# Windowed differential attention in an eight-sublayer kernel: q's spreads in the loop through the small banks and VectorE, and k with swapped k as one projection

## The chip, the cores and the metric

The kernel runs on one core of a Trainium2 chip. The metric is the device time of one launch in microseconds; the lower the better. A core has TensorE (PE: matmuls into PSUM, and PEld, its weight loads), VectorE (DVE), ScalarE (ACT), GpSimd (POOL) and SyncE (SP), which issues the transfers here. Each engine works through its own program in order and waits on semaphores that others raise. PSUM has eight banks of 128 x 512 float32; GpSimd has no work on them in this kernel.

## The reference

Four attention and four feed-forward sublayers follow each other on x of 1024 tokens x 256 features, each with a residual and a layer norm. Only the third one, with grouped keys and a window of 64, is touched by the change:

```python
q = (x @ Wq).reshape(b, s, N_HEADS, HEAD_DIM).transpose(0, 2, 1, 3)   # 16 heads of 16
k = (x @ Wk).reshape(b, s, N_KV, HEAD_DIM).transpose(0, 2, 1, 3)      # 4 heads of 16
v = (x @ Wv).reshape(b, s, N_KV, HEAD_DIM).transpose(0, 2, 1, 3)
q = q * cos + rotate_half(q) * sin
k = k * cos + rotate_half(k) * sin
q1, q2 = (q[..., :SUB], q[..., SUB:])                                  # SUB = 8
k1, k2 = (k[..., :SUB], k[..., SUB:])
a1 = jnp.einsum('bhqd,bhkd->bhqk', q1, k1) * scale                     # + window mask
a2 = jnp.einsum('bhqd,bhkd->bhqk', q2, k2) * scale                     # + window mask
p1, p2 = softmax(a1), softmax(a2)
diff = relu(p1 - lam[None, :, None, None] * p2)
diff = diff / (diff.sum(axis=-1, keepdims=True) + 1e-06)
out = jnp.einsum('bhqk,bhkd->bhqd', diff, v)
return out @ Wo
```

## The kernel before

**PSUM.** Three single banks, bank0 to bank2, form the small ring (`r_slot`): TensorE fills a slot and raises `r_full`, VectorE empties it and raises `r_free`; TensorE may be three slots ahead. Two pairs of banks, pair0 and pair1, form the big ring (`e_slot`): TensorE fills, ScalarE empties (`e_full`, `e_free`), two slots ahead. One bank, `pvb`, takes the products with v. Inside the loop of the windowed sublayer the two pairs are counted by `w_full` and `w_free` instead, over the items of `W_RING`.

**Rotation (items R).** The tokens are split in two halves of 512. `W_HALVES` lists six pieces: k for both halves, then q's two tiles of eight heads for the first half, then for the second. For each piece, `tile_rows(i, 0)` projects it and `tile_rows(i, 1)` projects it once more with swapped halves of each head (the weights lie side by side as wq, swapped wq, wk, swapped wk), each into a bank. VectorE multiplies the one by the cosine and the other by the sine (`rotate`, line 1237) and adds them (line 1241). For q these are 128 rows, for k 64. The sum is then cut into three bf16 parts: ScalarE rounds it (`highest`, line 922), VectorE subtracts and rounds again (`middle`, lines 1257 and 1258), GpSimd takes the rest (`lowest`, line 787). The buffers of the sum alternate between two.

**Spreads (items s).** `spread` (line 1695) multiplies the three parts by 0/1 selectors of 32 rows and so lays two heads (of q, or of k) out over 128 rows, in the pattern of parts that a bf16 product of float32 precision needs: six matmuls of 32 x 128 x 512 for two banks. Ahead of the loop, and in it, they take a slot of the big ring, and ScalarE copies both banks at once to bf16 (lines 937 and 944).

**The loop.** A unit is a block of 128 queries and a group of four heads; there are 8 x 4, in the order of `UNITS`. For unit k: TensorE fills both banks of a pair with the masked scores of a1 and a2 (S, lines 1742 and 1748); VectorE takes the negated maxima (line 1288); ScalarE writes the exponentials and their sums, four heads a bank (line 955); VectorE forms the ratio of the sums (`ratio`, lines 1269 and 1270); GpSimd scales the second half and subtracts (lines 804 and 807); three units later TensorE transposes the result into the small ring (uT, line 1757), from where VectorE takes it with a relu (line 1300). After four units TensorE multiplies with v (line 1774), ScalarE copies the sums (line 961), TensorE transposes them (line 1781) and VectorE divides (lines 1310 to 1312). The output projection, residual and norm of the first half (lines 1498 and 1316, 1493, 1056 to 1090) run in the later units.

**The order** is the list `W_BEFORE` and then `W_PLAN`, both from `windowed_plan`; every engine walks the same lists and takes its items. Before the loop: k's pieces, v of the half that is there first, the transposes of the other half of x (`x1`), the pieces of k and of the first half of q, then the spreads of k and of q's group 0. In the loop, behind the scores of units 0, 1 and 2: the two spreads of q's groups 1, 2 and 3 each; behind unit 3: v of the other half; behind 4 to 7: the pieces of q of the second half; behind 8 to 15: one spread each of the second half of q. On VectorE the ratio of unit k-1 stands behind the maxima of unit k, then the item of the list, then the relu of unit k-3.

## Time and profile before

| | us |
|---|---|
| median of 3 runs | 1169.01 |
| lowest and highest | 1168.03, 1169.27 |
| the profiled execution | 1170.22 |
| its span | 1168.5 |
| busy in the span: TensorE, VectorE, ScalarE, GpSimd | 1006.3, 699.4, 540.4, 331.8 |
| mean granted TensorE clock | 0.896 |

The rows below come from the one profiled execution. Times count from the start of the span. In a row of the timeline the first number is the start, the second the length in time (for a merged row from the first start to the last end), then engine, line, operation, the tile written <- the tiles read, partitions and elements, and how many; the brackets give how long the engine was idle before it and what ended that.
### The profile page before, as it was taken

Reading aid. Unit: us, or ns where it says so; the run is one execution under the profiler, and the core shown is the slowest. Engines: PE = TensorE matmul, PEld = TensorE weight load, DVE = VectorE, ACT = ScalarE, POOL = GpSimd, SP = SyncE. Lnnn points to the kernel's source line nnn. Section 1 sums busy time; section 2 is a strip of 40 time slices with the busy share of each in tenths; the row PEclk is TensorE's granted clock in tenths of the full one; section 3 lists DMA queues with packets and bytes.
Section 4 is the critical chain, followed back from the end, with each engine's and each line's share of the span. In section 5 each row is a group of like instructions: output and inputs, shape, how many; then the busy total and the mean of one; then the engine's idle time right before and its main releaser. Section 6 shows DMA issues by size and latency. Waiting matters only on the chain. (4 is left out here: it accounts for less than half of the span.)

```text
span 1168.5 us, 16473 instructions
## 1 busy us (share of the span) xinstructions
PE 1006.3 (86%) x5922; PEld 570.2 (49%) x5922; DVE 699.4 (60%) x1985; ACT 540.4 (46%) x1145; POOL 331.8 (28%) x464
## 2 busy tenths in 40 slices
PE   6999998788699886899999899997757988888785
PEld 2544454674254454437438444444444544445575
DVE  1667773776166794632432567777291688876665
ACT  3566655331768873210110556664304365555422
POOL 3211112331257773000000321112461154532223
PEclk8989998999576786899999889999877899999888
DMA  6000000103000000200000020000000000000000
GB/s 229 1 1 1 1 1 1 50 1 160 1 18 1 1 2 1 106 0 1 1 0 1 1 87 23 1 1 1 1 1 0 1 1 1 1 1 1 1 19 19
DMA packets 4325, 21.61 MB, mean 18 GB/s; under 512 B 377, under 2 KB 1657, under 8 KB 3220
## 3 DMA queue, kind: packets, MB, share of 16 engines
q1 hardware_dynamic: 4244, 20.55, 4.6%
q8 instruction: 48, 0.79, 0.3%
q14 instruction: 33, 0.27, 0.1%
HBM read 19.01 MB, written 1.05 MB: 17 GB/s over the span
## 5 line engine op out<-in xcount | busy, mean ns | idle before, releaser
L897 ACT ACTIVATE PB<-pair 128x1024 f32<-128x1024 f32 (+3 forms) x288 | 223.3, 812 | 135.3 <-PE pair L1621 133.8
L1139 DVE CUSTOM_DVE_ANT_0 junk<-bank,cst 128x128 bf16<-128x128 f32 (+3 forms) x384 | 171.3, 488 | 114.4 <-PE bank L1605 112.0
L730 POOL TENSOR_SCALAR_AFFINE_SELECT PB<-PB 128x256 f32<-128x256 f32 x192 | 79.0, 414 | 327.5 <-ACT PB L897 325.4
L1142 DVE TENSOR_REDUCE pmx<-bank 128x1 f32<-128x512 f32 x192 | 122.8, 685 | 55.9 <-PE bank L1605 54.9
L1605 PE MATMUL bank<-KO_r,QO_r 64*128 64x512 f32 (+3 forms) x576 | 140.2, 417 | 11.1 <-DVE A L1217 3.9
L1637 PE MATMUL pvb<-PB,V 128*32 128x512 f32 (+3 forms) x1152 | 125.3, 507 | 10.8 <-ACT PB L897 8.0
L1605 PEld LDWEIGHTS bank<-KO_r,QO_r 64*128 64x128 f32 x576 | 71.5, 189 | 113.6 <-DVE pmx L1139 38.9
L1617 PE MATMUL pair<-QO_r,KO_r 64*128 64x512 f32 (+3 forms) x576 | 114.4, 388 | 12.7 <-ACT PB L897 11.5
L736 POOL TENSOR_TENSOR parts_r<-y_f,parts_r 128x512 fp32r<-128x512 f32 x24 | 30.8, 1282 | 313.0 <-ACT parts_r L868 313.0
L955 ACT ACTIVATE KO<-pair,nm 128x128 f32<-128x128 f32 x256 | 90.1, 395 | 32.4 <-DVE nm L1288 32.3
L1621 PE MATMUL pair<-ms,sel_r 64*128 64x512 f32 (+3 forms) x576 | 101.1, 343 | 0.0
L1617 PEld LDWEIGHTS pair<-QO_r,KO_r 64*128 64x128 f32 x576 | 55.3, 186 | 62.9 <-ACT PB L897 50.1
L977 ACT ACTIVATE PB<-pair 128x512 f32<-128x512 f32 (+1 forms) x28 | 16.7, 597 | 125.3 <-PE pair L1493 125.3
L1056 DVE TENSOR_TENSOR X<-bank,X 128x256 f32<-128x256 f32 x56 | 23.7, 424 | 81.8 <-PE bank L1876 43.9
L804 POOL TENSOR_SCALAR KO<-KO,cc,cst 128x128 f32<-128x128 f32 x128 | 55.7, 450 | 50.0 <-DVE cc L1270 49.4
L1493 PE MATMUL pair<-xT,WA 128*128 128x512 f32 x96 | 61.6, 784 | 9.1 <-DMA WA<-in_w_att 7.7
L1288 DVE TENSOR_REDUCE nm<-pair 128x4 f32<-128x512 f32 x64 | 42.4, 686 | 31.4 <-PE pair L1748 31.0
L955 ACT ACTIVATION_READ_ACCUMULATOR KO<-pair,nm 128x1 f32 x256 | 60.3, 236 | 0.0
L1621 PEld LDWEIGHTS pair<-ms,sel_r 64*128 64x128 f32 x576 | 56.8, 187 | 3.8
L1493 PE MATMUL pair<-xT,WF 128*128 128x512 f32 (+1 forms) x112 | 56.8, 631 | 0.0
L1424 DVE TENSOR_TENSOR PB<-bank,PB 128x512 f32<-128x512 f32 (+1 forms) x28 | 19.4, 691 | 60.8 <-PE bank L1493 60.7
L1493 PE MATMUL bank<-xT,WF 128*128 128x512 f32 (+1 forms) x112 | 55.1, 616 | 0.0
(205 smaller groups left out, 1688.7 us busy)
## 6 DMA issues: line engine op xcount, KB each, us to landing
WF<-in_moe_gu SPq DMA_DIRECT2D x1, 3520.0 KB, 10.8
WA<-in_w_att SPq DMA_DIRECT2D x3, 1024.0 KB, 10.7
WF<-in_tern_w SPq DMA_DIRECT2D x1, 3072.0 KB, 9.8
V<-in_moe_d SPq DMA_DIRECT2D x1, 1792.0 KB, 7.5
xT<-in_xT SPq DMA_DIRECT2D x2, 512.0 KB, 5.8
X<-in_x SPq DMA_DIRECT2D x1, 1024.0 KB, 10.6
A<-in_rope SPq DMA_DIRECT2D x1, 1024.0 KB, 4.7
out<-X SPq DMA_DIRECT2D x2, 512.0 KB, 2.9
```

Of the source, the lines that this page charges most:

```text
L730: pool.affine_select(p2, p2, pattern=[[0, 2], [1, P]], compare_op=ALU.is_ge, fill=0.0, base=0, channel_multiplier=-1).then_inc(causal, 1)
L804: last = pool.tensor_scalar(e2[:, hh, :], e2[:, hh, :], cc[:, k % 4, 1, hh:hh + 1], lam, ALU.mult, ALU.mult)
L897: act.activation(pb[:, st % 2, 2 * i:2 * i + 2, 0:n], ps[:, :, 0:n], ACT.Exp, scale=scale)\
L955: last = act.activation(ew[k % EW][:, z, hh, :], slot[:, z, hh * P:(hh + 1) * P], ACT.Exp, bias=nm2[:, (2 * k + z) % 4, hh:hh + 1], accum_ ...
L1139: r_done(dve.tensor_tensor_reduce(junk[:, (r_used - 1) % 3, 0:n], ps[:, 0:n], tri[:, HALF - n:HALF], 1.0, LOWEST, ALU.add, ALU.max, accum_ ...
L1142: r_done(dve.tensor_reduce(to, ps[:, 0:n], AX.X, ALU.max))
L1288: dve.tensor_reduce(nm2[:, (2 * k + z) % 4, :], pair[(n // 2 - 1) % 2][:, z, :].rearrange("p (h n) -> p h n", h=HG), AX.X, ALU.max, negate ...
L1493: last = pe.matmul(ps, w(c), x(c), start=(c == 0), stop=(c == ND - 1))
L1605: pe.matmul(r_slot()[:, 0:n], qd[rows, TWO * g + i, t * P:(t + 1) * P], kd[rows, TWO * g + i, c * HALF:c * HALF + n], start=True, stop=Tru ...
L1617: pe.matmul(ps[:, j, 0:n], kd[rows, TWO * g + i, kb * P:(kb + 1) * P], qd[rows, TWO * g + i, q0:q0 + n], start=True, stop=False)
L1621: last = pe.matmul(ps[:, j, 0:n], sel_r[rows, 2 * TWO + i, :], ms[rows, b, q0 - qh * HALF:q0 - qh * HALF + n], start=False, stop=True)
L1637: last = pe.matmul(pvb[j * STRIP:(j + 1) * STRIP, q0 - qh * HALF:HALF], v_all[:, kb, g * HG + j, :], pb[:, st % 2, j, 0:n], start=(kb == 0 ...
```

## The change

1. In the loop, a spread of q takes two slots of the small ring instead of one of the big ring, and VectorE copies each bank (`q_rows`, two `tensor_copy`) instead of ScalarE the pair. The big ring holds only scores there. Scores that need freshly spread rows wait on `r_free`.
2. q's group 1 of the first half is spread ahead of the loop, also through the small ring. The other items move up by one unit: groups 2 and 3 behind units 0 and 1, v behind 2, the rotations behind 3 to 6, the spreads of the second half behind 7 to 14.
3. k and swapped k are projected by one matmul of 128 columns of weights instead of two of 64, for each half; VectorE multiplies rows 0 to 63 by the cosine and rows 64 to 127 by the sine into rows 0 to 63, with a wait between the two.
4. Ahead of the loop, the spreads of k's first half stand right behind the second projection of k, those of its other half behind q's pieces; `middle` of the last piece stands behind the copies of group 0.

```diff
--- before.py
+++ after.py
@@ -399,13 +399,16 @@
     def rows(side, g, half):
         return [("s", side, g, x, half) for x in range(TWO)]
 
-    before = [("R", 0, 0), ("R", 0, 1), ("v", W_SOON), ("x1",)] + [("R", i, k) for i in (1, 2, 3) for k in range(2)] \
-        + rows("k", 0, W_SOON) + rows("k", 0, W_LATE) + rows("q", 0, W_OUT)
-    late = {0: rows("q", 1, W_OUT), 1: rows("q", 2, W_OUT), 2: rows("q", 3, W_OUT), 3: [("v", W_LATE)],
-            4: [("R", 4, 0)], 5: [("R", 4, 1)], 6: [("R", 5, 0)], 7: [("R", 5, 1)]}
+    def q_rows(g, half):
+        return [("q", g, x, half) for x in range(TWO)]
+
+    before = [("R", 0, 1), ("v", W_SOON), ("x1",), ("R", 1, 1)] + rows("k", 0, W_SOON) \
+        + [("R", i, k) for i in (2, 3) for k in range(2)] + rows("k", 0, W_LATE) + rows("q", 0, W_OUT) + q_rows(1, W_OUT)
+    late = {0: q_rows(2, W_OUT), 1: q_rows(3, W_OUT), 2: [("v", W_LATE)],
+            3: [("R", 4, 0)], 4: [("R", 4, 1)], 5: [("R", 5, 0)], 6: [("R", 5, 1)]}
     for g in range(NG):
         for x in range(TWO):
-            late[8 + TWO * g + x] = [rows("q", g, W_END)[x]]
+            late[7 + TWO * g + x] = [q_rows(g, W_END)[x]]
     plan = []
     for k in range(len(UNITS) + 3):
         if k < len(UNITS):
@@ -432,7 +435,7 @@
 
 PLANS = {s: attention_plan(s) for s, kind in enumerate(SUBLAYERS) if kind == ATT}
 W_BEFORE, W_PLAN = windowed_plan()
-W_RING = [item for item in W_PLAN if item[0] in ("S", "s")]
+W_RING = [item for item in W_PLAN if item[0] == "S"]
 
 
 def w_banks(item):
@@ -469,7 +472,7 @@
 
     n = R_ATT + R_GLU
     for item in W_BEFORE + W_PLAN:
-        n += {"R": 1, "v": 1, "uT": 1, "accT": 1, "outT": ND, "proj": 1}.get(item[0], 0)
+        n += {"R": 1, "v": 1, "q": 2, "uT": 1, "accT": 1, "outT": ND, "proj": 1}.get(item[0], 0)
         if item == ("uT", gi):
             return n
 
@@ -938,10 +941,6 @@
                 for item in W_PLAN:
                     if item[0] == "R" and item[2]:
                         highest(item[1])
-                    if item[0] == "s":
-                        n = w_banks(item)
-                        act.wait_ge(w_full, n)
-                        act.activation(spread_to(item), pair[(n // 2 - 1) % 2][:, :, :], ACT.Copy).then_inc(w_free, 2)
                     if item[0] == "S":
                         k = item[1]
                         t, g = UNITS[k]
@@ -1231,15 +1230,26 @@
                     tile, half = W_HALVES[i]
                     rows, sc = (P, SUB ** -0.5) if tile < 2 else (KV * HD, 1.0)
                     x = w_buf[i % 2]
-                    if i >= 2 and k == 0:
+                    if i >= 2 and k == (tile == 2):
 
                         dve.wait_ge(w_lo, i - 1)
-                    r_done(dve.scalar_tensor_tensor(x[0:rows, k, :], r_slot()[0:rows, :], sc,
-                                                    rope[0:rows, k, half * HALF:(half + 1) * HALF], ALU.mult, ALU.mult))
+                    cols = slice(half * HALF, (half + 1) * HALF)
+                    if tile < 2:
+                        r_done(dve.scalar_tensor_tensor(x[0:rows, k, :], r_slot()[0:rows, :], sc,
+                                                        rope[0:rows, k, cols], ALU.mult, ALU.mult))
+                    else:
+                        ps = r_slot()
+                        step(dve.tensor_tensor(x[0:rows, 0, :], ps[0:rows, :], rope[0:rows, 0, cols], ALU.mult))
+                        r_done(dve.tensor_tensor(x[0:rows, 1, :], ps[rows:P, :], rope[rows:P, 1, cols], ALU.mult))
                     if k:
                         r_wait()
                         dve.tensor_tensor(x[0:rows, 0, :], x[0:rows, 0, :], x[0:rows, 1, :], ALU.add).then_inc(w_rows, 1)
                         turned.append(i)
+
+                def q_rows(g, x, half):
+
+                    for i in range(TWO):
+                        r_done(dve.tensor_copy(q_op[:, HG * g + TWO * i + x, half * HALF:(half + 1) * HALF], r_slot()[:, :]))
 
                 def v_tiles(half):
 
@@ -1278,7 +1288,10 @@
                     if item[0] == "v":
                         v_tiles(item[1])
                         middle(turned.pop())
-                middle(turned.pop())
+                    if item[0] == "q":
+                        if turned:
+                            middle(turned.pop())
+                        q_rows(*item[1:])
                 for item in W_PLAN:
                     if item[0] == "S":
                         k = item[1]
@@ -1294,6 +1307,8 @@
                         middle(turned.pop())
                     if item[0] == "R":
                         rotate(*item[1:])
+                    if item[0] == "q":
+                        q_rows(*item[1:])
                     if item[0] == "v":
                         v_tiles(item[1])
                     if item[0] == "uT":
@@ -1666,11 +1681,11 @@
                 def tile_rows(i, k):
 
                     tile, half = W_HALVES[i]
-                    rows, at = ((P, tile * P + k * D) if tile < 2 else (KV * HD, 2 * D + k * KV * HD))
+                    at = tile * P + k * D if tile < 2 else 2 * D
                     x_ready(half)
-                    w = w_att(s, at, rows)
+                    w = w_att(s, at, P)
                     ps = r_slot()
-                    over_width(ps[0:rows, :], lambda c: w[:, c, :],
+                    over_width(ps[:, :], lambda c: w[:, c, :],
                                lambda c: xT[:, c, half * HALF:(half + 1) * HALF]).then_inc(r_full, 1)
 
                 def v_tiles(half):
@@ -1686,17 +1701,25 @@
 
                 def spread(item, ps):
 
-                    _, side, g, x, half = item
-                    at = w_tile(item)
+                    side, g, x, half = item
+                    at = w_tile(("s",) + item)
+                    pe.wait_ge(ld_rope, 32)
                     pe.wait_ge(w_lo, at + 1)
+                    last = [None] * TWO
                     for k in range(3):
                         for i in range(TWO):
                             r0 = ((g % 2 * TWO if side == "q" else 0) + i) * STRIP
-                            last = pe.matmul(ps[:, i, :], sel_w[r0:r0 + STRIP, ("q", "k").index(side), k, x, :],
-                                             piece[r0:r0 + STRIP, at % 4, k, :], start=(k == 0), stop=(k == 2))
-                            if k == 2 and i < TWO - 1:
-                                yield last
-                    yield last
+                            last[i] = pe.matmul(ps[i], sel_w[r0:r0 + STRIP, ("q", "k").index(side), k, x, :],
+                                                piece[r0:r0 + STRIP, at % 4, k, :], start=(k == 0), stop=(k == 2))
+                    return last
+
+                q_at = {}
+
+                def q_rows(item):
+
+                    for last in spread(item, [r_slot()[:, :] for _ in range(TWO)]):
+                        last.then_inc(r_full, 1)
+                    q_at[item[1], item[3]] = r_used
 
                 for item in W_BEFORE:
                     if item[0] == "R":
@@ -1706,10 +1729,10 @@
                     if item[0] == "x1":
                         new_x(s - 1, halves_in(s)[1])
                     if item[0] == "s":
-                        pe.wait_ge(ld_rope, 32)
-                        for last in spread(item, e_slot()):
-                            pass
-                        last.then_inc(e_full, 1)
+                        ps = e_slot()
+                        spread(item[1:], [ps[:, i, :] for i in range(TWO)])[-1].then_inc(e_full, 1)
+                    if item[0] == "q":
+                        q_rows(item)
                 uT_at = {}
                 pe.wait_ge(cast_ready, 2)
                 pe.wait_ge(k_ones, 1)
@@ -1720,20 +1743,15 @@
                         tile_rows(*item[1:])
                     if item[0] == "v":
                         v_tiles(item[1])
-                    if item[0] == "s":
-                        n = w_banks(item)
-                        if n > 4:
-
-                            pe.wait_ge(w_free, n - 4)
-                        for last in spread(item, pair[(n // 2 - 1) % 2]):
-                            last.then_inc(w_full, 1)
+                    if item[0] == "q":
+                        q_rows(item)
                     if item[0] == "S":
                         k = item[1]
                         t, g = UNITS[k]
                         n = w_banks(item)
-                        if ("s", "q", g, TWO - 1, t // TH) in W_RING:
-
-                            pe.wait_ge(w_free, w_banks(("s", "q", g, TWO - 1, t // TH)))
+                        if (g, t // TH) in q_at:
+
+                            pe.wait_ge(r_free, q_at[g, t // TH])
                         for z in range(2):
                             if n > 4:
```

## Rows read from the trace of the kernel before

**Rows 1.** Stretches: length, busy (x) of PE, PEld, DVE, ACT, POOL, clock, DMA
```profile
300.20:329.40 29.20, 21.90 (x129) 9.76 (x129) 7.40 (x16) 17.41 (x70) 8.98 (x15) 0.50 0.01 2
329.40:348.10 18.70, 18.70 (x135) 9.06 (x135) 14.29 (x28) 12.69 (x66) 11.39 (x18) 0.87 0.10 26
348.10:385.20 37.10, 33.37 (x256) 15.78 (x252) 21.89 (x49) 31.32 (x139) 27.50 (x45) 0.68 0.01 2
385.20:413.20 28.00, 23.04 (x235) 13.56 (x237) 23.47 (x50) 23.63 (x130) 23.11 (x40) 0.87 0.01 2
...
299.02:301.20 2.18, 2.18 (x18) 0.96 (x18) 0.69 (x1) 1.42 (x2) 0.00 (x0) 0.50 0.04 8
...
334.56:335.98 1.42, 1.42 (x22) 0.69 (x20) 1.42 (x3) 0.00 (x0) 0.23 (x1) 1.00 0.00 0
```

**Rows 2.** Timeline ahead of the loop, 262 to 300 us
```profile
273.21 1.28 DVE L1237 SCALAR_TENSOR_TENSOR rest<-bank,A 64x512 f32<-64x512 f32 x2
...
275.24 0.63 ACT L922 ACTIVATE parts<-rest 64x512 bf16<-64x512 f32 x1 [16.91 <-DVE rest L1241]
...
276.89 12.15 PE L1493 MATMUL bank<-xT,WA 128*64 128x512 f32 x24 [2.56 <-ACT xT L834]
...
288.97 1.47 PE L1695 MATMUL pair<-parts,junk 32*128 32x512 bf16 x12
...
291.17 0.63 ACT L922 ACTIVATE parts<-y_f 128x512 bf16<-128x512 f32 x1 [3.00 <-DVE y_f L1241]
...
297.85 1.02 ACT L937 ACTIVATE QO<-pair 128x1024 bf16<-128x1024 f32 x1 [0.32 <-PE pair L1695]
```

**Rows 3.** Timeline of units 0 and 1, 299 to 308 us
```profile
299.02 0.59 PE L1742 MATMUL pair<-wmaskb,idb 128*128 128x512 bf16 x1 [1.21 <-ACT QO L937]
...
300.21 0.69 DVE L1288 TENSOR_REDUCE nm<-pair 128x4 f32<-128x512 f32 x1 [7.22 <-PE pair L1748]
...
301.21 1.46 PE L1695 MATMUL pair<-parts,junk 32*128 32x512 bf16 x6
...
303.69 1.06 ACT L944 ACTIVATE QO<-pair 128x1024 bf16<-128x1024 f32 x1
...
303.89 1.46 PE L1695 MATMUL pair<-parts,junk 32*128 32x512 bf16 x6 [1.22 <-ACT KO L955]
...
307.77 0.69 DVE L1288 TENSOR_REDUCE nm<-pair 128x4 f32<-128x512 f32 x1 [5.76 <-PE pair L1748]
```

**Rows 4.** Timeline of units 3 and 4, 322 to 330 us
```profile
322.90 0.69 DVE L1288 TENSOR_REDUCE nm<-pair 128x4 f32<-128x512 f32 x1 [5.49 <-PE pair L1748]
...
323.89 3.67 PE L1493 MATMUL bank<-WA,xT 128*128 128x64 f32 x16
...
329.45 0.69 DVE L1288 TENSOR_REDUCE nm<-pair 128x4 f32<-128x512 f32 x1 [0.31 <-PE pair L1748]
```

**Rows 5.** Timeline of VectorE: maxima of units 5, 8, 16 and 22
```profile
335.54 1.28 DVE L1288 TENSOR_REDUCE nm<-pair 128x4 f32<-128x512 f32 x2
...
348.13 1.27 DVE L1288 TENSOR_REDUCE nm<-pair 128x4 f32<-128x512 f32 x2
...
385.22 0.69 DVE L1288 TENSOR_REDUCE nm<-pair 128x4 f32<-128x512 f32 x1 [0.30 <-PE pair L1748]
...
403.25 1.47 DVE L1288 TENSOR_REDUCE nm<-pair 128x4 f32<-128x512 f32 x2
```

**Rows 6.** Lines 944 and 1316 over the span: durations in ns, min/median/max
```profile
L944 ACT ACTIVATE QO<-pair x14: 1023/1060/1135, 303.7 to 382.4; 128x1024 bf16<-128x1024 f32 x14
...
L1316 DVE COPY xT<-bank x2: 691/692/692, 407.0 to 407.9; 128x512 f32<-128x512 f32 x2
```

**Rows 7.** Timeline of TensorE: transposes, a spread, products with v
```profile
327.36 1.06 PE L1757 MATMUL bank<-cst,KO 128*128 128x128 f32 x4
...
365.71 0.82 PE L1695 MATMUL pair<-parts,junk 32*128 32x512 bf16 x6
...
381.20 1.94 PE L1774 MATMUL pvb<-PB,V 128*32 128x256 f32 x16
```

## The prediction, written before the changed kernel was run

> **What bounds the kernel now.** I read the views in this order: the slices of the page, to find the stage; the busy time of each engine in stretches of the stage; the timeline; and last the single lines that the change moves. Only the third sublayer, windowed differential attention, is touched. In the profiled execution VectorE starts the first maximum of unit 0, of 32, at 300.21 us. I call the start of a unit's first maximum (line 1288) the start of the unit. Starts read off the timeline are 300.21, 307.77, 322.90, 329.45, 335.54, 348.13, 385.22 and 403.25 us for units 0, 1, 3, 4, 5, 8, 16 and 22 [rows 3 to 5].
>
> So the stretch splits. Units 0 to 2 carry two spreads each and last (322.90 - 300.21) / 3 = 7.56 us. Unit 3 carries the late half of v and lasts 6.55 us. Units 4 to 7 carry the rotations and take 348.13 - 329.45 = 18.7 us together. Units 8 to 15 carry one spread each and take 37.1 us, 4.64 us each. Units 16 to 21 carry no spread and take 18.0 us, 3.0 us each. In all, 85.0 us pass up to unit 16.
>
> No engine is full in the first stretch. VectorE is busy 7.4 us of 29.2, ScalarE 17.4, GpSimd 9.0; TensorE shows 21.9 us, at a granted clock of 0.50, the lower of its two levels, 1.2 GHz [rows 1]. It is a chain of waits, and the timeline of one period shows it [rows 3]. TensorE issues the scores of unit 0 and the first spread (301.21), then has both big slots occupied. The second spread starts at 303.89, released by the last exponential of unit 0 (line 955); the scores of unit 1 then wait for the copy of the first spread on ScalarE (line 944, 303.69); their maximum starts at 307.77 after VectorE was idle for 5.76 us. The exponentials of unit 0 and the scores of unit 1 never overlap, because the spreads sit between them in the same two slots. Units 16 to 21 are the picture without that. There VectorE (23.5 us busy of 28.0), ScalarE (23.6) and GpSimd (23.1) are all near their limit [rows 1].
>
> **The change, part by part.**
>
> *The spreads of q leave the big slots.* Fourteen copies of 128x1024 on ScalarE, 1.06 us each at the median, 14.9 us in all, leave the loop; 28 copies of 128x512 come to VectorE, four of them ahead of the loop. That form, out of the same small banks, is on record at 0.69 us (line 1316) [rows 6]; two reads of this width behind each other took 1.28 us (the pair at 335.54 [rows 5]), so a spread costs VectorE 1.3 us and 28 copies some 18 us. In the slots, the scores of unit k+1 no longer queue behind a spread and behind the exponentials of unit k.
>
> *A unit with two spreads* (new units 0 and 1, at the low clock). TensorE issues scores for 2.18 us [rows 1]. The first spread takes 1.46 us [rows 3] and is readable about 1.5 us after its start. The second needs two banks of three, so it waits for the first of VectorE's copies, 0.65 us, and a handover of 0.15 us: it starts at +2.3 and is readable at +3.8. The scores of the next unit are issued behind it and are readable at +5.0. VectorE finishes its two copies at +5.1 and takes the maximum. With 0.75 us from the unit's start to the end of its scores a unit lasts 5.9 us, against 7.56. What is late next is VectorE's copy and the handover of the bank: three banks are too few for two spreads. Bounds for this unit: 5.2 us, were no bank ever waited for; 7.56, were nothing won.
>
> *A unit with v* (new unit 2). It is bound by TensorE: 2.18 us for the scores and 3.67 us for v [rows 4], at the low clock 5.85 by the issue; I take 5.7. Unit 3 now has the same two pieces and, ahead of the next scores, the first transposes of line 1757 [rows 7] besides; at unit 2 these are not due yet.
>
> *The units with rotations* (new 3 to 6) do what 4 to 7 do now. I take 19.2 us for 18.7, because the clock was 0.87 in that stretch [rows 1] and the first of them will still be at the low level, as unit 4 was.
>
> *The eight units with one spread each* (new 7 to 14). VectorE now has them as its load. Its busy time was 21.9 us for eight units [rows 1], 2.74 each; with 1.3 us of copies it is 4.05 us. GpSimd (27.5 us for eight, 3.4) and ScalarE (31.3 less 8 x 1.06, 2.9) lie below that. TensorE at the high clock needs at most 1.42 for the scores [rows 1], 0.82 for the spread, 1.06 for the transposes of line 1757 and a quarter of 1.94 for line 1774 [rows 7], 3.8 us; at the low clock 2.18 + 1.46 + 1.06 + 0.49 = 5.2 us. So the length p of such a unit is 4.05 us at the high clock, where VectorE sets it, and 5.2 us at the low clock, where TensorE does. In this place the clock was granted at 0.68 on average [rows 1], that is about a third of the time high, and units took 4.64 us. Fewer waits for slots should leave it high more often. I take p = 4.5 us, and keep 4.05 and 5.2 for the range.
>
> *Unit 15 carries no spread any more*: 3.3 us, a little over the 3.0 of units 16 to 21.
>
> *Ahead of the loop.* The merged projection of k takes 4 TensorE passes of each pair of 8 away. The first pair lies beside VectorE's normalisation, which holds everything until 273.21 [rows 2]: nothing is won. VectorE then does two tensor_tensor with a wait between them where it did two of line 1237 in 1.28 us; I take 0.1 us more, between 0 and 0.2, and it is on the path, as ScalarE's copy of x stands behind line 922, which waits for that sum (275.24). The second pair is the start of 24 passes in 12.15 us from 276.89; four passes go, and k's first two spreads, 12 matmuls in 1.47 us where they stand now [rows 2], move into the hole. So the rotations of q start where they do now. Bounds: 0 to 1.5 us won; I take 0, since the next thing late is VectorE's last sum, which releases ScalarE's line 922 at 291.17, and that chain of rotations is not shortened. Behind it ScalarE has four wide copies left where it had six (the last at 297.85), but q's second group is now spread there too: two spreads into three banks with a bank handover between. By the durations above the scores of unit 0 start about 298.8 instead of 299.02, and VectorE is free of its four copies about 300.2. So unit 0 starts where it does now; bounds 0.6 us earlier to 0.5 us later. What hides the four new copies is VectorE's idle 7.22 us ahead of unit 0's maximum [rows 3].
>
> *The sum* up to unit 16: 2 x 5.95 + 5.7 + 19.2 + 8 x 4.5 + 3.3 = 76.1 us, against 85.0: **8.9 us less**, with p = 4.05 12.5 less, with p = 5.2 3.3 less. The order of work is the same from unit 16 on, and GpSimd has no backlog at 4.5 us a unit, so I carry the gain to the end. The profiled execution took 1170.22 us (span 1168.5 and 1.7 around it), the median of the runs is 1169.01; 1170.22 - 8.9 = 1161.3, and 1.2 lower for the median: **1160.1 us**.
>
> *A rule against it.* In the low-clock stretches TensorE was in short bursts between waits for slots (1.22 us ahead of 303.89), and the clock stayed at 0.50 for 29 us [rows 1, 3]. "TensorE: Matmul & The Clock Gate" in the Trainium skill, section "A second HAM failure mode: psum-queue depth-cycling", says of 512-column bf16 matmuls that cycle through PSUM banks that TensorE idles briefly so often that its clock swings between the levels. The moved spreads have just that shape. By that rule p would lie at 5.2 and not at 4.5, and the gain at 3.3 us or less; it is the second and the third rival, priced from rows.
>
> **The rivals.**
>
> *The high clock holds* from the rotations to unit 16: p = 4.05, 12.5 us less, 1156.5 us. For it: TensorE would be needed for some 3.5 of every 4.05 us, more evenly than now, and in units 16 to 21 the clock held with less. Against it: the present stretch, as busy on paper, had 0.68.
>
> *The clock is low through units 7 to 14 and no longer*: p = 5.2, 3.3 us less, 1165.7 us.
>
> *The clock falls with the first small-bank spreads and stays low to the end of the loop.* This is the case that ends slower. Its place is units 7 to 31, its price p = 5.2 and then, for the 16 units without a spread, 2.18 + 1.06 + 0.49 and a quarter of an accumulator's transposes (0.27), 4.0 us against the 28.0 / 8 = 3.5 of now [rows 1]: 8 us lost against 3.3 won, 1173.7 us. It decides from the point where seven more of the late 16 units run at the low clock than now (7 x 0.5 us eat the 3.3). For it: clock 0.68 now in a stretch that never stood still long. Against it: clock 0.87 in units 16 to 23, where the change adds no work.
>
> *The change doesn't do what it says*, since VectorE takes its copies in program order: in units 0 and 1 the maximum of the next unit stands behind four copies, and the reciprocals (line 1269) on which GpSimd waits stand behind that. If the handover of banks cost 1.5 us and not 0.15, units 0 and 1 would give 2.7 us back; with p at VectorE's 4.05 and 1 us of waiting, 5.05, the eight units would give 4.4 back. That leaves 1.8 us, 1167.2 us.
>
> **How the numbers follow.** The forecast case (1158 to 1163.5) has 0.50; the high clock throughout (1154 to 1158) 0.19; the low clock in units 7 to 14 (1163.5 to 1166.7) 0.14; the copies in the way (1166.7 to 1171) 0.11; slower 0.06. The range that leaves two in ten out runs from 1155.5 to 1167.0. A measurement of this kernel tells 0.2%, 2.3 us, from no change. Faster by more than that 0.83, within it 0.11, slower 0.06.
>
> **What the profile of the changed kernel would show.** Right: unit 1 starts about 5.9 us after unit 0; the scores of unit 1 are issued before the exponentials of unit 0 have ended or straight after the spreads, with no wait for ScalarE; unit 3 starts near 318 us, unit 7 near 337 (317.8 + 19.2), unit 16 near 376 (337 + 36 + 3.3); VectorE's share in units 7 to 14 is over 0.85. Wrong in the first step: unit 0 starts after 301 us. Wrong in the second: VectorE waits for TensorE ahead of each pair of copies, while TensorE waits for a bank. Wrong in the third: a granted clock of 0.5 from unit 7 on, or unit 16 at 376 us and the end of the stage where it is now, which would say that GpSimd's chain and not the slots sets the later units.

## The result, and the profile after

| | before | after |
|---|---|---|
| median, us | 1169.01 | **1159.44** |
| lowest to highest, us | 1167.95 to 1170.16 (9 runs) | 1156.02 to 1166.00 (9 runs) |
| the profiled execution and its span, us | 1170.22, 1168.5 | 1156.02, 1154.2 |
| mean granted clock of that execution | 0.896 | 0.905 |

The ratio of the times is 0.9934, with a 95% interval of 0.9915 to 0.9952: the changed kernel is faster by 0.5 to 0.85%. The profiled execution is the fastest of the nine, so its times are read below stretch by stretch, and not as "14 us won". Two more executions of the same changed kernel were profiled (changed_again and changed_third below); where they differ from this one, the text says so.

The page of after first, the busy times over the whole span. VectorE rose from 699.4 to 715.9 us, ScalarE fell from 540.4 to 527.5, TensorE from 1006.3 to 993.1 (at another mean clock):

```profile
PE 993.1 (86%) x5914; PEld 566.8 (49%) x5914; DVE 715.9 (62%) x2013; ACT 527.5 (46%) x1131; POOL 331.9 (29%) x464
```

Then the stretches of after, cut at the starts of the units 0, 1, 2, 3, 7, 15 and 16 (in after the maxima are line 1301; columns as in [rows 1]):

```profile
297.64:303.53 5.89, 5.06 (x31) 1.60 (x30) 3.86 (x7) 2.90 (x16) 0.00 (x0) 0.50 0.00 0
303.53:309.42 5.89, 5.06 (x31) 1.60 (x30) 4.12 (x10) 2.90 (x16) 2.99 (x5) 0.50 0.00 0
309.42:315.05 5.63, 5.63 (x35) 4.40 (x34) 2.04 (x6) 2.91 (x16) 2.99 (x5) 0.50 0.00 1
315.05:334.32 19.27, 18.68 (x119) 9.04 (x118) 14.54 (x28) 12.74 (x66) 11.43 (x18) 0.84 0.10 26
334.32:370.07 35.75, 28.81 (x258) 14.07 (x258) 31.48 (x65) 23.90 (x130) 26.00 (x44) 0.81 0.01 2
370.07:372.61 2.54, 2.31 (x30) 1.33 (x30) 2.16 (x7) 2.17 (x14) 2.26 (x4) 1.00 0.03 6
```

Each row's second number is its length, and the third from its end the granted clock. Units 0 and 1 last 5.89 us each (7.56 before), the unit with v 5.63, the four with rotations 19.27 together, the eight with one spread 35.75, 4.47 each, and unit 15 2.54. Together they are 74.97 us against 85.0.

The timeline of after around unit 0 answers to [rows 3]:

```profile
297.64 0.68 DVE L1301 TENSOR_REDUCE nm<-pair 128x4 f32<-128x512 f32 x1
298.57 1.46 PE L1712 MATMUL bank<-parts,junk 32*128 32x512 bf16 x6
300.06 1.29 DVE L1252 CAST QO<-bank 128x512 bf16<-128x512 f32 x2 [0.70 <-PE bank L1712]
300.86 1.46 PE L1712 MATMUL bank<-parts,junk 32*128 32x512 bf16 x6 [0.83 <-DVE QO L1252]
302.25 0.61 PE L1760 MATMUL pair<-wmaskb,idb 128*128 128x512 bf16 x1
302.33 1.29 DVE L1252 CAST QO<-bank 128x512 bf16<-128x512 f32 x2 [0.97 <-PE bank L1712]
303.53 0.68 DVE L1301 TENSOR_REDUCE nm<-pair 128x4 f32<-128x512 f32 x1
```

Read the brackets. The second spread (300.86) waits 0.83 us for VectorE's first copy, which freed a bank. The scores of unit 1 (302.25) have no bracket at all: they follow the spread at once, where in [rows 3] they stood behind ScalarE's copy. VectorE's next maximum (303.53) has no bracket either: now VectorE comes late, with its second pair of copies, and not the scores.

### The profile page after: what moved, and what is told of

It reads as the page before. It is cut to its first block and busy times, and to the rows that moved or that the text cites. A ratio compares the mean times of both kernels' runs of the same rounds, so it can differ in the third digit from the quotient of the medians.

```text
span 1154.2 us, 16469 instructions
## 1 busy us (share of the span) xinstructions
PE 993.1 (86%) x5914; PEld 566.8 (49%) x5914; DVE 715.9 (62%) x2013; ACT 527.5 (46%) x1131; POOL 331.9 (29%) x464
## 5 line engine op out<-in xcount | busy, mean ns | idle before, releaser
L1141 DVE TENSOR_REDUCE pmx<-bank 128x1 f32<-128x512 f32 x192 | 122.6, 685 | 54.5 <-PE bank L1620 53.6
L954 ACT ACTIVATE KO<-pair,nm 128x128 f32<-128x128 f32 x256 | 90.2, 396 | 38.3 <-DVE nm L1301 36.9
L1632 PEld LDWEIGHTS pair<-QO_r,KO_r 64*128 64x128 f32 x576 | 55.4, 186 | 62.8 <-ACT PB L900 49.5
L807 POOL TENSOR_SCALAR KO<-KO,cc,cst 128x128 f32<-128x128 f32 x128 | 55.8, 450 | 37.8 <-DVE cc L1280 37.1
L837 ACT ACTIVATE xT<-pair 128x512 f32<-128x512 f32 x42 | 23.8, 594 | 54.3 <-PE pair L1513 54.3
```

The costliest lines, as they stand in the source:

```text
L807: last = pool.tensor_scalar(e2[:, hh, :], e2[:, hh, :], cc[:, k % 4, 1, hh:hh + 1], lam, ALU.mult, ALU.mult)
L954: last = act.activation(ew[k % EW][:, z, hh, :], slot[:, z, hh * P:(hh + 1) * P], ACT.Exp, bias=nm2[:, (2 * k + z) % 4, hh:hh + 1], accum_ ...
L1141: r_done(dve.tensor_reduce(to, ps[:, 0:n], AX.X, ALU.max))
L1632: pe.matmul(ps[:, j, 0:n], kd[rows, TWO * g + i, kb * P:(kb + 1) * P], qd[rows, TWO * g + i, q0:q0 + n], start=True, stop=False)
```

## The experiments

The kernels of each of the three groups ran on one chip with the kernel before.

| kernel | median, us | range (runs) | ratio to before, 95% interval |
|---|---|---|---|
| **chip one**, before | 1169.16 | 1167.87 to 1173.89 (18) | |
| changed_again | 1157.26 | 1156.25 to 1164.05 (6) | 0.9918 [0.9896, 0.9939] |
| k_alone | 1171.06 | 1164.21 to 1173.70 (12) | 1.0006 [0.9988, 1.0024] |
| q_alone | 1157.36 | 1156.23 to 1157.78 (4) | 0.9900 [0.9887, 0.9913] |
| g1_in_loop | 1171.82 | 1170.43 to 1175.57 (6) | 1.0027 [1.0015, 1.0039] |
| **chip two**, before | 1165.09 | 1159.32 to 1171.78 (20) | |
| narrow_copies | 1148.27 | 1143.26 to 1155.70 (6) | 0.9867 [0.9827, 0.9907] |
| double_copies | 1170.63 | 1164.20 to 1175.36 (12) | 1.0046 [1.0017, 1.0075] |
| mask_three | 1155.95 | 1154.40 to 1156.79 (6) | 0.9924 [0.9894, 0.9954] |
| v_later | 1154.17 | 1152.63 to 1160.96 (9) | 0.9925 [0.9895, 0.9955] |
| **chip three**, before | 1168.44 | 1164.09 to 1170.91 (25) | |
| changed_third | 1162.58 | 1157.07 to 1166.10 (12) | 0.9948 [0.9929, 0.9967] |
| big_ahead | 1166.97 | 1162.21 to 1170.14 (12) | 0.9990 [0.9971, 1.0009] |
| v_later2 | 1155.36 | 1149.58 to 1158.44 (6) | 0.9893 [0.9868, 0.9919] |
| later_two | 1161.82 | 1154.42 to 1163.78 (8) | 0.9937 [0.9913, 0.9961] |

### The two parts apart

changed_again and changed_third are the changed kernel itself. In this section the diffs show the lines that carry each experiment; where lines are left out, the text says which.

> The changed kernel as it stands, beside the three that follow. Its nine runs lay between 1156.0 and 1166.0 us with a median of 1159.4, those of the kernel before between 1168.0 and 1170.2. Theory: the spread comes from the granted clock of TensorE, which differs from run to run (0.894 to 0.905), so again 1156 to 1166, the long runs with the low clock, about 0.9 us for each 0.001 of mean clock. Rival: it was the chip, and the runs lie within 2 us here.

k_alone is the kernel before with the merged projection of k (point 3 of the change, with its `rotate` and `tile_rows`) and nothing else; all spreads stay where they were:

```diff
-    before = [("R", 0, 0), ("R", 0, 1), ("v", W_SOON), ("x1",)] + [("R", i, k) for i in (1, 2, 3) for k in range(2)] \
-        + rows("k", 0, W_SOON) + rows("k", 0, W_LATE) + rows("q", 0, W_OUT)
+    before = [("R", 0, 1), ("v", W_SOON), ("x1",), ("R", 1, 1)] + [("R", i, k) for i in (2, 3) for k in range(2)] \
+        + rows("k", 0, W_SOON) + rows("k", 0, W_LATE) + rows("q", 0, W_OUT)
```

> Only the merged projection of k and swapped k, in the kernel before, its order of spreads kept. Theory (the prediction's): the first pair of projections lies beside VectorE's normalisation and the chain of rotations on VectorE is no shorter, so unit 0 starts 0 to 1.5 us earlier and the time is within 1 us of 1169. Rival: the four passes taken out at the low clock (3.4 us) are on the path, unit 0 starts 3 us earlier and the time is 1166. Second rival: the extra wait and the second pass through VectorE cost 0.7 us and nothing is won, 1169.7.

q_alone is the changed kernel with k's two projections apart again (`rotate` and `tile_rows` are those of the kernel before; these lines are left out here):

```diff
-    before = [("R", 0, 1), ("v", W_SOON), ("x1",), ("R", 1, 1)] + rows("k", 0, W_SOON) \
+    before = [("R", 0, 0), ("R", 0, 1), ("v", W_SOON), ("x1",), ("R", 1, 0), ("R", 1, 1)] + rows("k", 0, W_SOON) \
```

> The changed kernel with k and swapped k projected apart again, as in the kernel before; all spreads as changed. Theory: the whole gain is here, 9 to 10 us under the kernel before, 1159 to 1160. Rival: a third of it belonged to the merged projection, 1162 to 1163.

The merge alone gives a ratio of 1.0006, and without it the change gives 0.9900 against 0.9918 with it, intervals that overlap. The merge is worth nothing that the medians can tell; **the gain is in q's spreads**. What the merge does at a given clock is less plain: in q_alone 27.20 us pass from the first rotation of k to unit 0 at a granted clock of 0.81, in after 25.69 at 0.80, but in changed_again and changed_third 28.7 at 0.68. The twelve runs of k_alone also spread over 9.5 us, with mean clocks from 0.886 to 0.900, so a small saving of the merge and a loss of clock may hide each other here; no run separates them. Unit 0 and the first stretch say the same. The rows are the first maximum of units 0 and 1 in k_alone, and the stretch of unit 0 in q_alone:

```profile
300.01 0.69 DVE L1294 TENSOR_REDUCE nm<-pair 128x4 f32<-128x512 f32 x1 [7.22 <-PE pair L1754]
307.58 0.69 DVE L1294 TENSOR_REDUCE nm<-pair 128x4 f32<-128x512 f32 x1 [5.77 <-PE pair L1754]
```

```profile
299.01:304.90 5.89, 5.06 (x31) 1.60 (x30) 3.87 (x7) 2.90 (x16) 0.00 (x0) 0.50 0.00 0
```

k_alone has units of 7.57 us with VectorE idle for 5.77 of them, as before; q_alone has the 5.89 of after.

### The ring and the order apart

The change moves q's spreads to other banks, and it also makes them one unit earlier. g1_in_loop keeps the first and undoes the second (left out: two lines that call `middle` for the last piece once the items ahead of the loop are done, as in the kernel before):

```diff
-        + ... + rows("q", 0, W_OUT) + q_rows(1, W_OUT)
-    late = {0: q_rows(2, W_OUT), 1: q_rows(3, W_OUT), 2: [("v", W_LATE)],
-            3: [("R", 4, 0)], 4: [("R", 4, 1)], 5: [("R", 5, 0)], 6: [("R", 5, 1)]}
+        + ... + rows("q", 0, W_OUT)
+    late = {0: q_rows(1, W_OUT), 1: q_rows(2, W_OUT), 2: q_rows(3, W_OUT), 3: [("v", W_LATE)],
+            4: [("R", 4, 0)], 5: [("R", 4, 1)], 6: [("R", 5, 0)], 7: [("R", 5, 1)]}
...
-            late[7 + TWO * g + x] = [q_rows(g, W_END)[x]]
+            late[8 + TWO * g + x] = [q_rows(g, W_END)[x]]
```

> The changed kernel with q's group 1 spread behind unit 0 again and everything behind it one unit later, as in the kernel before, but through the small banks. Theory: three units of 5.9 us instead of two, one plain unit of 2.5 to 3.3 less at the other end, unit 0 about 1 us earlier: 1.5 to 3 us slower than the changed kernel, 1161 to 1162.5. Rival (the small banks are all that counts): no difference, 1159.5. Second rival (the place of group 1 is all that counts, the banks little): 1166 or more.

The theory and the first rival missed. The second rival came true with its 1166 or more: without the earlier order the small banks give the whole kernel nothing, and it is 0.15 to 0.39% slower than the kernel before. The timeline around unit 0 shows what the theory had left out:

```profile
301.48 1.46 PE L1714 MATMUL bank<-parts,junk 32*128 32x512 bf16 x6 [0.83 <-DVE QO L1252]
302.95 1.29 DVE L1252 CAST QO<-bank 128x512 bf16<-128x512 f32 x2 [0.98 <-PE bank L1714]
304.30 0.61 PE L1762 MATMUL pair<-wmaskb,idb 128*128 128x512 bf16 x1 [1.35 <-DVE QO L1252]
305.51 0.69 DVE L1303 TENSOR_REDUCE nm<-pair 128x4 f32<-128x512 f32 x1 [1.27 <-PE pair L1768]
```

The two copies (302.95) are those of the group that unit 1 asks about. TensorE stands idle for 1.35 us until both are done, issues the scores, and VectorE stands idle for 1.27 us until the first of them can be read. Up to 301.48 this is the changed kernel's timeline, wait for wait; from there the unit is 1.4 us longer, 7.31 in all (298.20 to 305.51), and there are three such units instead of two. In the changed kernel the rows that are being copied belong to the unit after the next, so that copy and scores run beside each other.

This wait takes most of the ring's gain in such a unit, but it does not make the kernel slower than before: 7.31 us is still less than 7.56, and ahead of the loop 24.39 us pass from the first rotation of k to unit 0 (273.81 to 298.20) where before has 27.00. What is lost is lost behind it. Units 8 to 15 last 42.6 us at a granted clock of 0.57, where before has 37.1 at 0.68 [rows 1]:

```profile
344.50:387.10 42.60, 37.82 (x256) 17.21 (x252) 32.57 (x66) 24.30 (x131) 27.44 (x45) 0.57 0.00 1
```

All six runs have a mean clock of 0.885 to 0.891, and the runs of before on that chip 0.892 to 0.899. Why the clock is lower is not shown; the loss of this kernel as a whole can't be put down to the wait alone.

big_ahead is the other half, the earlier order with the old banks: the kernel before with the lines below (left out: a constant that counts the uses of the big ring ahead of the loop, two more):

```diff
-        + rows("k", 0, W_SOON) + rows("k", 0, W_LATE) + rows("q", 0, W_OUT)
-    late = {0: rows("q", 1, W_OUT), 1: rows("q", 2, W_OUT), 2: rows("q", 3, W_OUT), 3: [("v", W_LATE)],
-            4: [("R", 4, 0)], 5: [("R", 4, 1)], 6: [("R", 5, 0)], 7: [("R", 5, 1)]}
+        + rows("k", 0, W_SOON) + rows("k", 0, W_LATE) + rows("q", 0, W_OUT) + rows("q", 1, W_OUT)
+    late = {0: rows("q", 2, W_OUT), 1: rows("q", 3, W_OUT), 2: [("v", W_LATE)],
+            3: [("R", 4, 0)], 4: [("R", 4, 1)], 5: [("R", 5, 0)], 6: [("R", 5, 1)]}
...
-            late[8 + TWO * g + x] = [rows("q", g, W_END)[x]]
+            late[7 + TWO * g + x] = [rows("q", g, W_END)[x]]
```

> Order alone: the kernel before, k's projections and the big ring with ScalarE's copies as they were, but q's group 1 is spread ahead of the loop and every later item stands one unit earlier, as in the changed kernel. Theory (order and ring are both needed): the next scores no longer wait for rows just copied, but the second spread of a unit still waits in the big ring for the exps, and the scores behind it for a bank that a copy of 1.06 us must clear; units 0 and 1 last 6.0 to 7.0 us (changed 5.9, before 7.56), and ScalarE keeps two copies of a pair in each, so the time is 3 to 7 us under the kernel before, 3 to 7 over the changed one. Rival one (the order alone is the gain): within 2 us of the changed kernel, units 0 and 1 at 5.9. Rival two (the ring alone holds the units): units 0 and 1 stay at 7.3 to 7.6 us; the kernel is within 2 us of the kernel before.

Its timeline around unit 0:

```profile
302.62 0.69 DVE L1288 TENSOR_REDUCE nm<-pair 128x4 f32<-128x512 f32 x1 [9.84 <-PE pair L1748]
303.61 1.46 PE L1695 MATMUL pair<-parts,junk 32*128 32x512 bf16 x6
306.10 1.06 ACT L944 ACTIVATE QO<-pair 128x1024 bf16<-128x1024 f32 x1
306.30 1.46 PE L1695 MATMUL pair<-parts,junk 32*128 32x512 bf16 x6 [1.23 <-ACT KO L955]
307.69 0.61 PE L1742 MATMUL pair<-wmaskb,idb 128*128 128x512 bf16 x1
308.91 0.69 DVE L1288 TENSOR_REDUCE nm<-pair 128x4 f32<-128x512 f32 x1 [4.50 <-PE pair L1748]
```

The scores of unit 1 follow their spread at once (307.69, no bracket), so the order has done its part; but the second spread still waits 1.23 us for the last exponential of unit 0. Units 0 and 1 last 6.29 us, as the theory said, and from unit 0 to unit 16 pass 80.1 us (302.62 to 382.74), 4.9 less than before. The time missed it: the interval includes 1. Ahead of the loop the two spreads more go through the big ring, with two copies of 1.02 us more on the path, and 29.55 us pass from the first rotation of k (line 1237, at 273.07) to unit 0 where before had 27.00 [rows 2, 3]: 2.5 us lost. Another 3.3 are lost from unit 16 to unit 31, 58.0 us at a granted clock of 0.79 against 54.7 at 0.84; the kernels do the same work there.

That leaves a table of two by two. The ratio is that of the whole kernel; the other rows come from the profiled executions, of which the changed kernel has three. "Ring alone" has the merged k besides.

| | neither | ring alone | order alone | both |
|---|---|---|---|---|
| ratio to before | 1 | 1.0027 | 0.9990 | 0.9934, 0.9918, 0.9948 |
| a unit with two spreads, us | 7.56 | 7.31 | 6.29 | 5.89 |
| first rotation of k to unit 0, us (clock) | 27.0 (0.81) | 24.4 (0.81) | 29.5 (0.78) | 25.7 (0.80), 28.7 (0.68), 28.7 (0.68) |
| unit 0 to unit 16, us (clock) | 85.0 (0.66) | 88.9 (0.62) | 80.1 (0.65) | 75.0 (0.75), 77.3 (0.68), 77.4 (0.68) |

**Neither part alone makes the kernel faster by its median; both together do.** In the unit with two spreads the shares can be read: the order gives 1.27 us of the 1.67, and the ring 0.25 by itself and 0.40 on top of the order. With the order alone the ring holds the unit at 6.3, with the ring alone the data hold it at 7.3. In the whole kernel each part also changes what lies around these units, and the clock with it, so the ratios are no sum of waits. At one mean clock the order alone does save something: the five runs of big_ahead at 0.900 to 0.903 took 1162.2 to 1163.9 us, six of before at 0.901 on the same chip 1164.6 to 1165.3.

### What sets a unit with one spread

double_copies changes VectorE's copies alone. narrow_copies shortens them and, so that no uncopied columns are read, lets the scores take their queries from the 128 columns that are copied; its attention is therefore another one:

```diff
-                        r_done(dve.tensor_copy(q_op[:, HG * g + TWO * i + x, half * HALF:(half + 1) * HALF], r_slot()[:, :]))
+                        ps = r_slot()
+                        r_done(dve.tensor_copy(q_op[:, HG * g + TWO * i + x, half * HALF:half * HALF + P], ps[:, 0:P]))
...
-                                                     q_op[rows, g * HG + hh, at:at + WIN], kw_op[rows, g, at:at + P],
+                                                     q_op[rows, g * HG + hh, at - t % TH * P:at - t % TH * P + WIN], kw_op[rows, g, at:at + P],
```

```diff
-                        r_done(dve.tensor_copy(q_op[:, HG * g + TWO * i + x, half * HALF:(half + 1) * HALF], r_slot()[:, :]))
+                        ps = r_slot()
+                        to = q_op[:, HG * g + TWO * i + x, half * HALF:(half + 1) * HALF]
+                        step(dve.tensor_copy(to, ps[:, :]))
+                        r_done(dve.tensor_copy(to, ps[:, :]))
```

> The changed kernel, but VectorE copies only the first 128 of the 512 columns of each spread bank (0.28 us instead of 0.68), and the scores of every block of a half take their queries from those 128 columns, so the attention is that of other queries; all else runs in full. Theory: VectorE sets the units with one spread, and its first copy sets the second spread of units 0 and 1: units 0 and 1 5.9 to 5.5 us, units 7 to 14 from 4.47 to about 4.0 (TensorE and GpSimd next), 4 to 5 us less than the changed kernel. Rival: TensorE at its low clock and the chain through GpSimd set them, 1 us less at most.

> The changed kernel with every spread bank copied twice by VectorE, the second copy behind a wait. Theory: VectorE is the bound of units 7 to 14, 1.3 to 1.4 us more for each of eight, and about 2 us more for each of units 0 and 1: 13 to 15 us slower than the changed kernel, 1173. Rival: VectorE has slack there, since TensorE at its low clock needs 5.2 us: 5 to 8 us slower.

mask_three adds to TensorE alone: the product that lays the mask into each bank of scores is issued three times, each time from zero, so that the result stays the same.

```diff
-                            pe.matmul(ps..., idb[:, :], wmaskb..., start=True, stop=False)
+                            for again in range(3):
+                                pe.matmul(ps..., idb[:, :], wmaskb..., start=True, stop=(again < 2))
```

> The changed kernel with the matmul that lays the mask into each bank of scores issued three times instead of once (it starts the sum anew each time, so the result is unchanged): 4 more matmuls of 128x128x512 a unit, 0.85 us of TensorE at the high clock, 1.7 at the low one. Theory: TensorE is on the path in units 0 to 3 and close to it in 7 to 14, so 7 to 12 us slower than the changed kernel. Rival: the added work brings the granted clock of the loop's first units from 0.5 to 1.0, a unit with two spreads falls from 5.9 to 4.8 us, v from 3.67 to 1.84: up to 5 us faster than the changed kernel.

One row of each, units 7 to 14, in this order (compare 334.32:370.07 of after):

```profile
332.86:358.43 25.57, 22.89 (x254) 11.82 (x256) 24.00 (x66) 22.80 (x126) 23.14 (x39) 1.00 0.01 2
```

```profile
339.60:382.81 43.21, 34.72 (x258) 16.56 (x258) 41.04 (x82) 24.36 (x131) 27.59 (x45) 0.66 0.01 1
```

```profile
335.28:367.85 32.57, 30.44 (x297) 14.47 (x296) 30.79 (x65) 24.07 (x131) 25.65 (x43) 1.00 0.01 2
```

A unit lasts 3.20, 5.40 and 4.07 us; after has 4.47. VectorE is busy for 0.94, 0.95 and 0.95 of these three stretches, and 0.88 of the one of after. With the full copies and the clock at 1.00 the unit is 4.07 us, VectorE's load and little more; copies of 128 columns (0.28 us each at the median, for 0.68) take 0.87 off it at the same clock, though mask_three has its additional products on TensorE as well. So **at the high clock VectorE's copies set these units**. At the low clock TensorE does. The timeline of TensorE in after, from unit 10 to unit 12, at the low clock:

```profile
348.25 0.61 PE L1760 MATMUL pair<-wmaskb,idb 128*128 128x512 bf16 x1
348.79 0.64 PE L1766 MATMUL pair<-KO,QO 64*64 64x128 bf16 x8
349.36 1.46 PE L1712 MATMUL bank<-parts,junk 32*128 32x512 bf16 x6
350.75 1.11 PE L1775 MATMUL bank<-cst,KO 128*128 128x128 f32 x4
351.66 0.63 PE L1760 MATMUL pair<-wmaskb,idb 128*128 128x512 bf16 x1
...
355.28 1.94 PE L1792 MATMUL pvb<-PB,V 128*32 128x256 f32 x16
357.15 1.12 PE L1775 MATMUL bank<-cst,KO 128*128 128x128 f32 x4
358.06 0.63 PE L1760 MATMUL pair<-wmaskb,idb 128*128 128x512 bf16 x1
```

There is not one wait in it, and its units last 4.53 us, or 6.31 with the products with v.

For whole kernels, narrow_copies stands at 0.9867 / 0.9934 of the changed kernel, about 8 us less (over two chips, by their ratios), more than the 4 to 5 of its theory, and its first two units last 5.49 us each, the 5.5 expected. double_copies stands at 1.0046 / 0.9934, about 13 us more, as expected; but its first two units last 6.83 and 7.11, about 1 us more each and not 2, and some of the rest lies ahead of the loop, where 30.9 us pass from the first rotation to unit 0.

mask_three bears out its rival: with more work on TensorE the granted clock was 1.00 from 304 us to the last unit with a spread, and its six runs lie within 2.4 us where those of the changed kernel spread over 8 to 10 (on other chips). It gave the gain back in the units without a spread: from unit 15 to unit 31 pass 62.8 us at a clock of 0.97, for 57.1 at 0.85 in after.

### The products of 64 columns later

The high clock comes back, in before and after alike, in the unit behind v. v_later puts the first projections of q's second half, 512 columns wide, ahead of v, 64 columns wide:

```diff
-    late = {0: q_rows(2, W_OUT), 1: q_rows(3, W_OUT), 2: [("v", W_LATE)],
-            3: [("R", 4, 0)], 4: [("R", 4, 1)], 5: [("R", 5, 0)], 6: [("R", 5, 1)]}
+    late = {0: q_rows(2, W_OUT), 1: q_rows(3, W_OUT), 2: [("R", 4, 0)], 3: [("R", 4, 1)], 4: [("v", W_LATE)],
+            5: [("R", 5, 0)], 6: [("R", 5, 1)]}
```

> The changed kernel with the first two projections of q's second half behind units 2 and 3 and v behind unit 4 (now v behind 2, the projections behind 3 and 4). Theory: in both traces the clock rose some 3.5 us into the first wide projection of the loop, so it rises about 5.6 us earlier, v takes 1.84 us instead of 3.67 and a unit's scores 1.42 instead of 2.18: 2 to 3 us faster than the changed kernel, 1156.5 to 1157.5. Rival: the clock rises at the same time whatever the order, no difference.

> The changed kernel once more, to compare the other three with on one chip. Both theories: a ratio to the kernel before of 0.990 to 0.995, with runs spread over some 8 us that follow the mean granted clock.

> The changed kernel with the first two projections of q's second half behind units 2 and 3 and v behind unit 4, so that products of 64 columns come after the wide ones. Theory (the clock rises some us earlier, and what that gives is lost again in a later low stretch): within 2.5 us of the changed kernel. Rival (the earlier rise is kept): 3 us or more under the changed kernel on this chip.

On chip two v_later has a ratio of 0.9925, [0.9895, 0.9955], which lies among the changed kernel's own on the other chips (0.9918 to 0.9948) and tells the two apart from before but not from each other. Its theory put the rise of the clock some 3.5 us into the first wide projection; by the rows of before and after it came 4.0 and 5.4 us behind that projection's start.

v_later2 is v_later once more, beside the changed kernel on one chip. There the median is 1155.36 us against 1162.58, and the intervals of the two ratios, 0.9868 to 0.9919 and 0.9929 to 0.9967, don't meet. **On this chip this order beats both kernels.** Units 3 to 6, first of the changed kernel (changed_third), then of v_later2, and behind each the stretch of units 7 to 15:

```profile
319.80:338.50 18.70, 17.99 (x119) 8.67 (x118) 14.41 (x28) 12.73 (x66) 11.45 (x18) 0.87 0.11 27
338.50:379.80 41.30, 36.74 (x288) 17.30 (x288) 33.98 (x71) 27.07 (x147) 30.14 (x50) 0.67 0.01 2
```

```profile
317.20:333.10 15.90, 15.65 (x131) 8.83 (x130) 13.89 (x29) 12.66 (x66) 11.49 (x18) 1.00 0.13 32
333.10:371.40 38.30, 31.16 (x288) 15.40 (x288) 33.62 (x71) 25.94 (x142) 28.40 (x47) 0.82 0.01 2
```

Units 3 to 6 have the clock at 1.00 throughout and last 15.9 us instead of 18.7 (19.27 in after), with v in the place of one projection. The 38.3 us behind them are those of after (35.75 + 2.54), so some 3 us are the order's own. The rest of what separates the two profiled executions lies where their work is the same: 3.0 us from the first rotation to unit 0 (28.7 at a clock of 0.68 in changed_third, 25.7 at 0.80 in v_later2), 2.9 in units 7 to 15, and 1.4 from unit 16 on to unit 31. The theory on record, that the gain would be lost again later, is not borne out. It came from the profiled run of v_later, where units 7 to 15 took 41.3 us (334.6 to 375.9); that is a matter of the single run, as 41.3 and 38.3 for the changed kernel show.

later_two adds the mask product a second time to that order (`range(2)` in the diff of mask_three).

> The same order as the run before it, and each mask product issued twice instead of once (the result is the same, 64 more products of 128x512). Theory (the filler costs 0.2 to 0.4 us a unit where TensorE is waited for, and pays it back by a higher clock): mean clock above 0.91, a spread of runs under 4 us, and a median 1 to 5 us under the changed kernel's. Rival (the filler pays for nothing): a median at or above the changed kernel's, clock as there.

It missed: 1161.82 us, no faster than the changed kernel and slower than the same order without filler, with runs 9 us apart. Units 0 to 2 had the low clock nearly throughout all the same, and there two mask products more a unit cost 0.7 us each unit (19.5 us for three in place of 17.3):

```profile
302.70:322.20 19.50, 17.84 (x89) 5.54 (x90) 10.51 (x20) 9.04 (x48) 6.02 (x10) 0.53 0.00 0
```

## Why the prediction was right, point by point

**The two-spread unit.** Predicted 5.9 us (5.95 in the sum), measured 5.89, and built as the prediction built it: spread at +0.93 from the maximum, second spread at +3.22 released by VectorE's copy, scores behind it without a wait, VectorE's copies last. But the condition under which that holds was not in the prediction. It credited the unit to the small banks, and "the scores of the next unit are issued behind it" was taken for granted; g1_in_loop shows that this needs the rows to be a unit ahead, and that without it the ring gives 0.25 us a unit (7.31 for 7.56). big_ahead shows that the order, which the sum never priced, gives most of it (6.29). The sum is also loose by itself: its own steps add up to 5.85, the text says 5.9 and the sum 5.95.

**The unit with v and those with rotations.** 5.7 and 19.2 predicted, 5.63 and 19.27 measured. Both were carried over from rows of before, with TensorE's work at its clock.

**The eight units with one spread.** p = 4.5 predicted, 4.47 measured, a mean of two regimes as it was argued: the ends were 4.05 for the high clock and 5.2 for the low. The runs put 4.07 at the first (mask_three at clock 1.00), and units 9 to 11 of after, nearly all at the low clock, took 15.28 / 3 = 5.09 us (343.94 to 359.22). The granted clock was 0.81 there and not 0.68, but only in this execution: changed_again and changed_third have 36.46 us, 4.56 a unit, at 0.68, the clock of before. So "fewer waits should leave it high more often" is not borne out, and at the same clock these eight units gained 0.6 us (37.1 to 36.46) and not 1.1. VectorE's share was 0.88, over the 0.85 named as the sign.

**A rule against it.** The clock in the loop did not fall with the small-bank spreads: 0.81 here for 0.68 (and 0.68 in the two other executions), 0.50 as before in units 0 to 2, 0.84 as before from unit 16 to unit 31. The cycling through banks that "TensorE: Matmul & The Clock Gate" of the Trainium skill, section "A second HAM failure mode: psum-queue depth-cycling", describes did not cost the change its gain. The clock does swing between the levels within the eight units, but it did so in the kernel before as well (0.68), and no run shows that the cycling is the reason.

**Unit 15** was mis-sized: 2.54 us, not 3.3, with the clock at 1.00. In the two other executions it took 4.78.

**Ahead of the loop** the prediction said nothing won, with bounds of 0.6 us earlier and 0.5 later. From the first rotation of k on VectorE to unit 0 it was 25.69 us in after (271.95 to 297.64), against 27.00, 1.3 us less, outside the bounds; in changed_again and changed_third it was 28.7, 1.7 us more, outside them on the other side. In these two, unit 0 starts at 302.3 and 302.4 us: "unit 0 starts after 301 us" was the prediction's own sign of being wrong in its first step. The rows on the way in after:

```profile
281.33 7.13 PE L1508 MATMUL bank<-xT,WA 128*128 128x512 f32 x16
...
290.60 0.63 ACT L925 ACTIVATE parts<-y_f 128x512 bf16<-128x512 f32 x1 [3.00 <-DVE y_f L1246]
```

The chain of rotations was 0.7 us later than before, not even (290.60 is 18.65 us behind the first rotation, 291.17 in [rows 2] was 17.96); k's spreads now stand ahead of q's pieces, which is the likely reason. From there to unit 0 it took 7.04 us instead of 9.04: that is the term that was mis-sized. Two of ScalarE's six wide copies had moved ahead, and the copies of q's second group, which were to fill the time again, ran beside the last of ScalarE's. And this term depends on the clock, which the prediction left out of it: it was granted at 0.80 in after, 0.81 in before and 0.68 in changed_third, where the same pieces took longer and the stretch lasted 28.7 us:

```profile
281.19 2.74 PE L1712 MATMUL pair<-parts,junk 32*128 32x512 bf16 x12
283.86 8.72 PE L1508 MATMUL bank<-xT,WA 128*128 128x512 f32 x16
```

**The sum.** 76.1 us up to unit 16 predicted, 74.97 measured, 10.0 less than before instead of 8.9. It was carried to the end, as predicted: from unit 16 to unit 31 pass 54.5 us (372.61 to 427.15) against 54.7. The profiled span is 14.3 us shorter: these 10.0, 0.1 up to unit 31, the 1.3 us above, 1.3 us of an earlier start ahead of k's first rotation (271.95 for 273.21), and 1.6 us behind the last unit's start; the last two no experiment separates. In the three executions of the changed kernel the terms of the sum came out like this:

| | predicted | after | changed_again | changed_third | before |
|---|---|---|---|---|---|
| first rotation of k to unit 0, us | 27.0 | 25.7 | 28.7 | 28.7 | 27.0 |
| unit 0 to unit 16, us | 76.1 | 75.0 | 77.3 | 77.4 | 85.0 |
| unit 16 to unit 31, us | 54.7 | 54.5 | 58.1 | 56.0 | 54.7 |
| mean clock of the execution | | 0.905 | 0.897 | 0.894 | 0.896 |

The second row, which the change was made for, is 7.6 to 10.0 us less in all three. The other two move by 3 and by 3.5 us between executions of one kernel.

**The median** of 1160.1 was predicted and 1159.44 measured. The profiled time itself was forecast at 1161.3 and came out at 1156.02. The step from there to the median assumed that the profiled run of after would stand to its median as that of before did. It did not: it was 3.4 us faster than the median. That the forecast fell so near is in part luck; on the other chips the changed kernel won 11.9 and 5.9 us by its medians.

## What to carry to other kernels

A ring of buffers that two kinds of work share is relieved in full only when both the slot and the data are a step ahead. Price the two halves apart, each with what it does ahead of the loop: here the order gave most of the unit, and the other banks kept its early copies from costing 2.5 us. Where a unit is set by one engine at the high clock and by TensorE at the low one, price it for both levels and look at what stands at the edges of the low stretch; moving a narrow product behind wide ones shortened four units by 3 us for two edited lines, on one chip the whole kernel by more. Profile a kernel more than once where its runs spread: one execution alone would have said that the stretch ahead of the loop was won and that the clock of the eight units had risen, and two others show neither.
